# Unread TensorE products ahead of two waits in a four-layer cross-attention kernel

## The reference, cut to what matters

```
for layer in 0..3:
    q = x @ Wq                     # 20 heads of 8
    k, v = ctx @ Wk, ctx @ Wv      # of the layer
    p = softmax(q k^T / sqrt(8))   # per head, 77 or 73 text tokens
    o = p v                        # layer 3 adds a second softmax over 4 image tokens,
                                   # whose scores need p (ctx ctx^T) p and norms
    x = o @ Wo + bias + x
```

## Time and profile before

| | us |
|---|---|
| median of 3 runs (2081.03, 2085.03, 2081.18) | 2081.18 |
| the profiled execution, its own time | 2084.85 |
| its span, first to last instruction | 2083.1 |
| PE busy | 2018.8 (97%) |
| PE weight loads busy | 1727.1 (83%) |
| DVE busy | 1477.4 (71%) |
| ACT busy | 1113.1 (53%) |
| POOL busy | 460.7 (22%) |

### The profile page before, as it was taken

The page is one execution under the profiler, slowest core; times in us unless marked ns, Lnnn a source line. Parts: engine busy times, 40 slices in busy tenths (PEclk is TensorE's granted clock), DMA queues, the critical chain, the costliest instruction groups (busy, mean ns, idle before and its releaser), DMA issues.

```text
span 2083.1 us, 69547 instructions
## 1 busy us (share of the span) xinstructions
PE 2018.8 (97%) x26906; PEld 1727.1 (83%) x26906; DVE 1477.4 (71%) x4457; ACT 1113.1 (53%) x2916; POOL 460.7 (22%) x872
## 2 busy tenths in 40 slices
PE   5899999999999999999999999999999999999975
PEld 4788888888888888888888888888888888888864
DVE  3367777777777777777777777777777777777754
ACT  1355555555555555555555555555555555555531
POOL 1122222222122122222222212222222221222210
PEclk9999999999999999999999999999999999999986
DMA  4112111211211211112111111111211112111000
GB/s 123 57 36 52 48 49 49 55 47 44 55 48 43 56 47 51 49 46 56 45 55 49 42 56 47 50 50 47 53 47 53 49 45 55 48 43 42 23 13 5
DMA packets 107969, 100.47 MB, mean 48 GB/s; under 512 B 42060, under 2 KB 84412, under 8 KB 107644
## 3 DMA queue, kind: packets, MB, share of 16 engines
q1 hardware_dynamic: 105740, 94.93, 16.8%
q10 hardware_dynamic: 1904, 1.09, 0.3%
HBM read 34.13 MB, written 5.41 MB: 19 GB/s over the span
## 4 chain that ended last, share of the span: by engine, by line
PE 95%; DVE 2%; issue 2%; ACT 1%; DMA 0%; ACTq 0%; POOLq 0%; DVEq 0%; POOL 0%
PE ps_s L774 13%; PE ps_c L852 12%; PE ps_s L808 10%; PE ps_c L919 8%; PE ps_k L676 6%; PE ps_k L872 6%; PE ps_q L753 5%; PE ps_c L908 5%; PE ps_s L824 5%; PE ps_k L701 5%; PE ps_k L877 4%; PE ps_c L885 4%; PE ps_c L924 3%; PE ps_k L704 2%; PE ps_q L838 2%
## 5 line engine op out<-in xcount | busy, mean ns | idle before, releaser
L1187 DVE TENSOR_REDUCE top<-ps_s 128x6 f32<-128x462 f32 (+3 forms) x1024 | 510.5, 543 | 33.6 <-PE ps_s L774 32.5
L1072 ACT ACTIVATE p_t<-ps_s 116x512 f32<-116x512 f32 (+1 forms) x768 | 376.1, 544 | 76.1 <-PE ps_s L808 69.7
L774 PE MATMUL ps_s<-k_blocks,q_sb 32*128 32x231 f32 (+1 forms) x3584 | 318.8, 375 | 2.4 <-ACT p_t L1072 1.9
L852 PE MATMUL ps_c<-p_t,v_rows 116*27 116x128 f32 (+1 forms) x7168 | 280.6, 278 | 6.0 <-ACT p_t L1072 5.2
L1227 DVE TENSOR_TENSOR weighted<-ps_k,probs 128x462 f32<-128x462 f32 (+1 forms) x256 | 142.1, 555 | 182.4 <-PE ps_k L877 180.3
L1418 POOL TENSOR_TENSOR k_blocks<-k_sb,mask_k 128x231 f32<-128x231 f32 x384 | 211.8, 573 | 263.8 <-PE ps_s L808 243.8
L774 PEld LDWEIGHTS ps_s<-k_blocks,q_sb 32*128 32x128 f32 x3584 | 214.8, 184 | 45.7 <-issue 7.6
L852 PEld LDWEIGHTS ps_c<-p_t,v_rows 116*27 116x27 f32 (+1 forms) x7168 | 209.5, 106 | 41.2 <-issue 18.6
L808 PE MATMUL ps_s<-q_sb,k_blocks 32*116 32x128 f32 (+1 forms) x5376 | 222.6, 284 | 8.7 <-DVE probs L1202 8.2
L1100 ACT ACTIVATE o_t<-ps_c 128x256 f32<-128x256 f32 x256 | 98.4, 384 | 236.5 <-PE ps_c L908 171.4
L1427 POOL TENSOR_TENSOR weighted<-weighted 128x720 f32<-128x720 f32 x64 | 92.8, 1450 | 593.6 <-DVE weighted L1227 593.6
(11 more groups left out here) (118 smaller groups left out, 3745.2 us busy)
## 6 DMA issues: line engine op xcount, KB each, us to landing
v_rows<-v_img SPq DMA_DIRECT2D x128, 227.4 KB
context<-in_ctx SPq DMA_DIRECT2D x64, 336.0 KB, 3.0
q_sb<-top_t SPq DMA_DIRECT2D x549, 6.0 KB
v_rows<-v_img SPq DMA_DIRECT2D x64, 115.2 KB
v_rows<-v_img SPq DMA_DIRECT2D x64, 112.2 KB
v_rep<-v_dram SPq DMA_DIRECT2D x64, 50.0 KB
gram<-g_img SPq DMA_DIRECT2D x64, 46.3 KB
q_sb<-top_t SPq DMA_DIRECT2D x183, 2.0 KB
```

The source lines that it names most:

```text
L774: ins = pe.matmul(ps_s[:, z * 512 + j * GT:z * 512 + j * GT + n], q_sb[c % 3][lo:lo + QUAD, j * S:(j + 1) * S], k_blocks[c % 3][lo:lo + QU ...
L852: ins = pe.matmul(ps_c[t % 2][32 * (g % 4):32 * (g % 4) + UC, g // 4 * S:(g // 4 + 1) * S], v_rows[b % NC][0:n, v:v + UC], p_t[c % 3][0:n, ...
L1072: act.activation(to, source, ACT.Exp, scale=SCALE).then_inc(p_ready, 1)
L1187: dve.tensor_reduce(top_at(c, z), s.rearrange("p (h t) -> p h t", t=T)[:, :, 0:n], AX.X, ALU.max).then_inc(s_top, 1)
```

## The change

A helper `spin(to, n)` issues n products of the identity with itself, 128 x 128 each, into a PSUM region that nothing reads. It is called in two places:

- in `product`, six of them, between the wait for `o_ready` and the wait for `p_ready`, in steps t below 16 and above 256. With the units that exist, these are steps 2, 6, 7, 10, 11, 12, 14 and 15, and 257, 259, 260, 261, 264, 265 and 269;
- in `exponents`, sixteen of them, ahead of its first wait, where t (the unit plus one) is above 256 and unit t isn't a layer 3. With the units that exist, this is step 258 alone.

Together these are 106 products, or 212 records. The hardware loop is not touched, nor is any other engine's program.

```diff
         @block.tensor
         def _(pe):
+            def spin(to, n):
+
+
+                for i in range(n):
+                    pe.matmul(to, ident[:, :], ident[:, :], start=True, stop=True)
+
...
                 t = c + 1
+                if t > 4 * B and not ip(t):
+                    spin(ps_s[:, 3 * 512 + 384:4 * 512], 16)
                 if moved(c):
                     pe.wait_ge(top_ready[c % 3], raised(k, MOVED_IN[c % 3], c, per=64, first=0))
                 else:
...
                 pe.wait_ge(v_ready[b % NC], loads(k, b, NC, per=4))
                 pe.wait_ge(x_ready, raised(k, out, t - 4 + LAG))
                 pe.wait_ge(o_ready, raised(k, exists, c - 2))
+                if t < T0 - 4 or t > 4 * B:
+                    spin(ps_c[t % 2][:, 384:512], 6)
                 pe.wait_ge(p_ready, raised(k, exists, c, per=4))
                 for kind, gs in PWAVES:
```

## The result

| | before | after |
|---|---|---|
| median of the launches taken together | 2083.83 us (6, from 2081.03 to 2090.5) | 2091.06 us (6, from 2090.95 to 2093.4) |
| ratio | | 1.0036, 95% interval 1.002 to 1.0053 |
| profiled execution, own time | 2084.85 | 2091.07 |
| its span | 2083.1 | 2089.3 |
| mean granted clock | 0.983 | 0.990 |

The change makes the kernel slower by 0.36% (7.5 us at the ratio). The forecast was 2094.0 within 2086 to 2104. Between the two profiled executions the difference is 6.2 us, in the time as in the span.

The account below looks back on a forecast made before the run. PE, busy for 97% of the span and running in program order, bounds the kernel. Costs of 30.0 us less clock gains of 19.3 add 10.7 to 2084.85, 2095.6; half of 3.67 off gives 2094, range 2086 to 2104.

Parts of the forecast that it names:

- a sum of 10.7: Whole kernel: costs of the products, 30.0 us, less what a higher clock gives back, 19.3 us.
- The price: Each added product: 0.32 us at the high clock, taken from L919; six cost 1.92 us, or 3.45 at 1.2 GHz.
- the products are cheaper: Rival, all added products: 0.24 us each, from L676, giving 2085 us; chance 0.12.
- Nine uncovered places: Steps 7, 11, 12, 14, 15, 257, 260, 261, 265: no wait covers the six; 9 x 1.92 = 17.3 us.
- The prediction's sign of a wrong price: In the timeline: runs of 12 records taking under 1.4 us would show the price wrong.
- The estimate of 0.22: Each added product, from the Trainium skill: 0.22 us, at which costs and gains cancel and the time stays as before.
- The small terms: Partly covered sixes: steps 2, 264, 269 cost 1.7, 1.7, 2.7 us; step 10 1.25; step 6 0.2; step 259 free.
- The clock: Six low-clock stretches of start and end: work sped up from 1.2 GHz gives back 19.3 us together.
- The stretch I counted half, at 109: Start, 109.4 to 112.8, under steps 13 and 14: half of 3.40 x 0.44, 0.8 us given back.
- The sixteen: Step 258, ahead of L808 at 1981.98: they fill no wait and move the whole chain by 5.1 us.
- The middle: The 1840 us between start and end: nothing there swallows a delay, so the start's is passed on whole.
- The half of 3.67: Profiled execution before, 3.67 us above the runs' median: half of that taken off, from 2095.6 to 2094.

Follow-up runs that it names:

- the five covered steps: Against the kernel before: six products only in steps 2, 6, 259, 264 and 269, and no sixteen; 2072.9 us, ratio 0.995.
- e6_transposes: Against the changed kernel: two transposes of the identity in place of each product; 2089.87 us, ratio 1.0021 to the kernel before.
- e7_twelve: Against the changed kernel: twelve instead of six products in steps 7, 11, 12, 14 and 15; 2097.96 us, ratio 1.0057 to the kernel before.

## Why the prediction was right, and where its terms were off

**Direction, size, cause.** It forecast a slowdown because most of the products stand where PE has no wait, and this is what the runs show: of 106 products, the 30 of the five covered steps make the kernel 10 us faster, and the other 76 turn that into 7.5 us slower. The median came out at 2091.06 for 2094.0. Between the profiled executions the difference was 6.2 us for a sum of 10.7, and 7.5 by the ratio. Both sides of the sum were too large, the costs by 6.6 us and the gains by 1.7, so the errors cancel in part; that the time came out within 3 us is to that extent luck.

**The price** was mis-sized, and it is the term that carries most of the error. I took 0.32 us from L919, the row of the same shape, and it was 0.24 at the full clock and 0.48 for 0.575 at half. The trace of the kernel before has another row of the same shape, which I didn't use:

```profile
86.74 0.61 PE L753 MATMUL ps_q<-x_in,wq_lead 128*128 128x128 f32 x4
87.19 1.21 PE L676 MATMUL ps_k<-context,wk 128*128 128x154 f32 x8
```

These are two products in 0.45 us, 0.22 each. Record by record (not shown), L753 goes on by 0.11 us each time, and so does the run of twelve. In L919, at 2002.02, two of the four steps are 0.11 and two are 0.21: the one behind its first record and the one from its last to L924. A run of four bears these two tenths on two products, a run of twelve bears one on six. My row thus held costs of the change to the neighbouring instructions, not of the product; what in the neighbours makes them was not tried.

The rival "the products are cheaper" had named 0.24, scaled from L676, and gave it 0.12. Nine uncovered places then cost 9 x 1.43 = 12.9 us for the predicted 17.3, the sixteen 3.7 for 5.1. The prediction's sign of a wrong price, runs of 12 under 1.4 us, was missed by a hair at 1.43, although the price was off by a quarter. The estimate of 0.22 that the prediction makes from the Trainium skill (TensorE: Matmul & The Clock Gate, Back-to-back issue gap; FP8 and Floating Point Precision, TensorE Precision Notes) agrees with the 0.223 of a further product in a run; not so the conclusion that the time would then be that of before, because the clock gave back less too.

**The small terms.** Step 2: 2.86 - 1.74 = 1.1 for 1.7. Step 264: 2.86 - 1.71 = 1.2 for 1.7. Step 269: 2.59 - 0.78 = 1.8 for 2.7. Step 259 was free, as forecast: its wait went from 3.07 to 1.53. Step 6 cost 2.74 - 1.74 = 1.0 for 0.2 and step 10 2.37 - 0.67 = 1.7 for 1.25, since both ran into half the clock. In all some 23.4 us for 30.0.

**The clock** gave back 23.4 - 5.8 = 17.6 us for the predicted 19.3. This is what is left when the 5.8 us of the table (the 6.2 between the launches, less the 0.4 of the late start) are taken from the costs, and not a measurement of its own. Behind steps 2 and 259 it came as forecast. At 55 the fall was not prevented but cut from 10.2 to 3.5 us. The stretch I counted half, at 109, did go, and another came at 80 instead. From step 269 on, I had counted all of 14.2 us of PE's time, and 4.4 of it (2066.6 to 2071.8) ran at half again.

**The sixteen** did what the prediction says, to the place: L808 later by their own 3.7 us, the same 4.09 and 8.73 us of waits as before, and alone they are 3.5 us of the 7.5.

**The middle** swallows nothing: +3.2 us at its entry, 4.5 ahead of the sixteen (not shown), of which step 257 brought 1.4, and of the 5.2 us that the doubled sixes add at step 15, 5.1 arrive at step 257.

**The half of 3.67** that I took off for the launch's place among the runs was too much: with six launches the profiled one lies 2084.85 - 2083.83 = 1.0 us above the median. The spread that it was worked out from is real (before: 2080.7 to 2090.2 in the 63 launches of the three sets). The six launches of the changed kernel scatter less, 2090.95 to 2093.4, but that its products make the clock's course more alike is not shown: with products or transposes at the same places, `e6_transposes` scatters from 2083.31 to 2093.19 and `e7_twelve` from 2093.42 to 2100.12.

## What to carry to other kernels

Work without a reader paid here where TensorE stood waiting, for all or most of its length, for something that doesn't depend on it. Put ahead of a wait whose end it can't delay, it is free and can raise the clock for the work behind. Its price is taken from a long run of its own kind, full clock and half clock apart: in L919's run of four records the changes to other instructions make up a third of the time. Ask of every such place what the profile gives as idle time there, and leave the rest out: here that turned 0.36% slower into 0.5% faster. A delay in the first microseconds of a kernel whose one engine is then always busy is paid in full at the end.

## What the runs showed of the hardware that I had not expected

- A float32 product of 128 x 128 weights and 128 columns costs 0.22 us within a run at the full clock, in L753 with other weights for each product as in the run of the identity. The 0.32 of L919 holds two tenths of a microsecond, at its first record and behind its last, that are paid once a run and not once a product.
- 128 x 128 transposes raise the clock as products do: with twelve of them in place of six products the kernel takes 2089.87 us, not some 2103, and behind step 2 the L682 takes 1.21 us instead of 2.26. The Trainium skill (TensorE: Matmul & The Clock Gate, Part 4: PE-mode transpose) says that they don't count; the runs differ from it.
- Products on 32 of the 128 rows take TensorE as long (1.53 us for twelve records, against 1.43) and did not bring the full clock behind steps 2 and 6. The kernel takes 2114.06 us, 23 us more than with 128 rows.
